# The opening loads, late values and second stacks of the projection reordered, and the last attention output finished in the next program

## The reference

```python
Q, K, V = split_heads(x @ Wq.T), split_heads(x @ Wk.T), split_heads(x @ Wv.T)
Q, K = rope(Q), rope(K)
probs = softmax(where(causal, Q @ K.T / sqrt(16), -inf))
x = layernorm(x + (probs @ V).merge_heads() @ Wo.T)

xf = layernorm(x) * ln_w + ln_b
expert = argmax(xf @ router_w); score = sigmoid(max(xf @ router_w))
xe = xf * score                                 # of the chosen expert only
routed = (silu(xe @ gate_w[e]) * (xe @ up_w[e])) @ down_w[e]
shared = (silu(xf @ sh_gate) * (xf @ sh_up)) @ sh_down
x = layernorm(x + (x + routed + shared))
```

## Time and profile before

| | us |
|---|---|
| median of 3 runs | 997.4 (996.0 to 997.84) |
| the profiled execution, its own time | 995.47 |
| its span from first to last instruction | 993.7 |
| busy PE, share of the span | 960.4, 97% |
| busy DVE | 738.8, 74% |
| busy ACT | 456.5, 46% |
| busy POOL | 364.4, 37% |

### The profile page before, as it was taken

How to read it: one execution, slowest core, us unless ns; L and a number is a source line. 1 busy time by engine, 2 the same in 40 slices (tenths; PEclk the granted TensorE clock), 3 DMA queues, 4 the chain that set the end, 5 groups by cost and what they waited for, 6 DMA issues and landing times. The chain is left out here.

```text
span 993.7 us, 19060 instructions
## 1 busy us (share of the span) xinstructions
PE 960.4 (97%) x6032; PEld 555.1 (56%) x6032; DVE 738.8 (74%) x1819; ACT 456.5 (46%) x639; POOL 364.4 (37%) x484
## 2 busy tenths in 40 slices
PE   7998899999999999999998799999999999999996
PEld 3556433343334333343333256666665899999996
DVE  4887899999999999999995556666666455655654
ACT  2453276667776676667766611222122233233231
POOL 7995232222222222222223124433334234433434
PEclk9999799999999999999999999999999999999999
DMA  8788434556665464755710187333334232222221
GB/s 295 179 234 197 75 55 61 60 76 84 95 93 75 61 102 61 103 75 73 156 18 8 17 258 244 87 81 81 80 115 167 70 93 79 74 80 78 77 72 44
DMA packets 176542, 100.17 MB, mean 101 GB/s; under 512 B 133856, under 2 KB 163168, under 8 KB 173120
## 3 DMA queue, kind: packets, MB, share of 16 engines
q1 hardware_dynamic: 162928, 72.66, 39.0%
q0 software_dynamic: 4944, 13.77, 3.9%
q10 hardware_dynamic: 8576, 12.58, 3.8%
HBM read 65.86 MB, written 32.70 MB: 99 GB/s over the span
## 5 line engine op out<-in xcount | busy, mean ns | idle before, releaser
L1037 ACT ACTIVATE probs<-scores_ps 128x1024 f32<-128x1024 f32 (+3 forms) x384 | 289.9, 807 | 118.4 <-PE scores_ps L978 115.7
L297 DVE TENSOR_REDUCE maxima<-max_ps 128x1 f32<-128x512 f32 (+2 forms) x352 | 228.2, 682 | 31.4 <-PE max_ps L255 20.8
L255 PE MATMUL max_ps<-k_stack,q_stack 96*128 96x512 bf16 (+3 forms) x768 | 224.1, 333 | 3.3 <-DVE maxima L292 0.5
L1140 POOL TENSOR_SCALAR_AFFINE_SELECT probs<-probs 128x512 f32<-128x512 f32 x128 | 81.3, 635 | 304.2 <-ACT probs L1037 303.4
L978 PE MATMUL scores_ps<-q_stack,k_stack 99*128 99x512 bf16 (+3 forms) x768 | 183.5, 328 | 3.5 <-PEq L355 1.7
L998 PE MATMUL out_ps<-probs,v_ones 128*32 128x512 f32 (+3 forms) x1536 | 163.6, 498 | 2.7 <-POOL probs L1140 2.2
L255 PEld LDWEIGHTS max_ps<-k_stack,q_stack 96*128 96x128 bf16 x768 | 74.5, 97 | 157.1 <-DVE maxima L297 58.7
L292 DVE CUSTOM_DVE_ANT_0 masked_out<-max_ps,mask_wide 128x384 bf16<-128x384 f32 (+1 forms) x256 | 149.2, 621 | 9.8 <-PE max_ps L255 6.1
L1425 ACT ACTIVATE silu<-gate_ps 128x512 f32<-128x512 f32 x71 | 42.4, 597 | 237.9 <-PE gate_ps L1344 140.6
L978 PEld LDWEIGHTS scores_ps<-q_stack,k_stack 99*128 99x128 bf16 x768 | 67.2, 98 | 66.2 <-ACT probs L1037 15.0
L1689 POOL DMA_INDIRECT out<-final,target_i x39 | 50.3, 1291 | 100.6 <-DVE final L1624 99.3
(11 more groups left out here) (163 smaller groups left out, 1211.9 us busy)
## 6 DMA issues: line engine op xcount, KB each, us to landing
k_stack<-k_parts SPq DMA_DIRECT2D x96, 128.0 KB, 4.3
q_stack<-q_parts SPq DMA_DIRECT2D x96, 128.0 KB, 7.4
q_parts<-parts SPq DMA_DIRECT2D x32, 192.0 KB, 3.2
k_parts<-parts SPq DMA_DIRECT2D x32, 192.0 KB, 3.2
sums_in<-expert_sums SPq DMA_DIRECT2D x39, 136.0 KB, 2.1
rows_in<-expert_rows SPq DMA_DIRECT2D x156, 32.0 KB
x_t<-in_x_cols SPq DMA_DIRECT2D x8, 512.0 KB, 11.2
heads_rows<-heads_out SPq DMA_DIRECT2D x128, 32.0 KB, 1.9
```

Source lines behind the costliest of these rows:

```text
L255: last = nc.tensor.matmul(part, self.q_stack[:ROWS, u.slot, h0 + k, t * P:(t + 1) * P], self.k_stack[:ROWS, u.slot, h0 + k, chunk * BLOCK: ...
L297: nc.vector.tensor_reduce(self.maxima[:, u.slot, chunk, h0:h0 + heads, t], self.bank("piece", u.i, n)[:, :heads * keys].rearrange("p (h k) ...
L1037: nc.scalar.activation(probs[:, s % RING, 2 * pair:2 * pair + 2, n0:], scores_ps[:, pair, :, n0:], ACT.Exp).then_inc(exp_done, 1)
L1140: nc.gpsimd.affine_select(out=tile, in_=tile, compare_op=ALU.is_ge, fill=0.0, base=0, pattern=[[0, GROUP], [1, P]], channel_multiplier=-1) ...
```

## The change

It touches the projection in five places, and the seam between `attend` and `feed`.

- First loads. x block 0 and Wq are loaded in halves by contraction chunk c, x and Wq in turn, each half with a semaphore of its own; then Wk, the half of the tables for Q, Wv, the half of the tables for K. `pair` runs its loops with c outside, and pair 0 waits for each half by itself. PE first does 8 matmuls of 128 columns on a zeroed tile `warm`, which DVE sets.
- ACT copies out values 7 and 8 before `mid(14)`, not between `high(15)` and `mid(15)`.
- The 12 stack loads of the second unit go out two at a time behind the stores of pairs 9 to 14, not behind all stores.
- DVE leaves the last 2 of the second unit's 13 early reductions to the start of `attend`.
- `send_neg` sends each of the three parts when it is made.
- `turn_out`, `normalise` and `store_heads` of the last output, and `make_tanh` and `make_score` of block 0, move to the start of `feed`. `final`, a tile of `feed`, now lies in `out_t`.

```diff
@@ send_neg
-        sp.wait_ge(self.neg_split, 4 * (u.i + 1))
-        for n in range(PARTS):
+        for n, steps in enumerate((1, 3, 4)):
+            sp.wait_ge(self.neg_split, 4 * u.i + steps)
@@ project
-    stacks_until = [min(max(0, 2 * (k - 2)), m.STACK_DMAS) if k > 2 else 0 for k in range(PAIRS)]
+    stacks_until = [min(max(0, 2 * (k - 2)), 2 * m.STACK_DMAS) for k in range(PAIRS)]
...
-            load_x(0)
-            sp.dma_start(w_qk[:, 0], io["Wq"].rearrange("(c p) o -> p c o", p=P)).then_inc(wq_in, 16)
-            sp.dma_start(tables[:, 0], io["tables"][:, 0]).then_inc(tables_in[0], 16)
+            for c in range(DC):
+                sp.dma_start(x_t[:, 0, c], x_cols[:, c, :BLOCK]).then_inc(x_half[c], 16)
+                sp.dma_start(w_qk[:, 0, c], io["Wq"][c * P:(c + 1) * P]).then_inc(wq_half[c], 16)
+            sp.dma_start(w_qk[:, 1], io["Wk"].rearrange("(c p) o -> p c o", p=P)).then_inc(wk_in, 16)
+            load_tables(0)
             sp.dma_start(w_v[:], io["Wv"].rearrange("(c p) o -> p c o", p=P)).then_inc(wv_in, 16)
-            sp.dma_start(w_qk[:, 1], io["Wk"].rearrange("(c p) o -> p c o", p=P)).then_inc(wk_in, 16)
+            load_tables(1)
...
-            m.load(sp, second, range(m.STACK_DMAS))
+            m.load(sp, second, range(stacks_until[-1] - m.STACK_DMAS, m.STACK_DMAS))
...
-                for e in range(2):
-                    for c in range(DC):
+                for c in range(DC):
+                    if k == 0:
+                        pe.wait_ge(x_half[c], 16)
+                        pe.wait_ge(wq_half[c], 16)
+                    for e in range(2):
...
+            pe.wait_ge(warm_made, 1)
+            for _ in range(8):
+                nc.tensor.matmul(v_ps[:, 0, 0, :P], warm[:], warm[:], start=True, stop=True)
...
-                late = k == PAIRS - 1
-                for n in values_after[k][:2] if late else values_after[k]:
+                for n in values_after[k] if k < PAIRS - 1 else ():
                     keep_v(n)
+                if k == PAIRS - 2:
+                    for n in values_after[PAIRS - 1][:2]:
+                        keep_v(n)
                 mid(k)
...
+            nc.vector.memset(warm[:], 0.0).then_inc(warm_made, 1)
...
-            m.reduce(dve, second, range(m.EARLY))
+            m.reduce(dve, second, range(m.EARLY - 2))
@@ attend
-            store_heads(Unit.number(UNITS - 1), 1)
...
-            f.make_tanh(act, 0, 0, 0)
...
+            m.reduce(dve, Unit.number(1), range(m.EARLY - 2, m.EARLY))
             each_unit(step)
             f.find_place(dve, 0, 0, 0)
-            turn_out(Unit.number(UNITS - 1), 1)
-            normalise(Unit.number(UNITS - 1), 1)
-            f.make_score(dve, 0, 0, 0)
@@ feed
-            for c in range(2):
-                sp.wait_ge(f.heads_stored[c], 16 * GROUP * UNITS)
+            sp.wait_ge(f.heads_stored[0], 16 * GROUP * (UNITS - 1))
+            sp.wait_ge(f.heads_stored[1], 16 * GROUP * (UNITS - 1))
...
                     f.load(sp, 2 * batch + 2, batch + 1, 0)
+                if isinstance(batch, int) and batch == 0:
+                    f.store_heads(sp, Unit.number(UNITS - 1), 1)
+                    sp.wait_ge(f.heads_stored[0], 16 * GROUP * UNITS)
+                    sp.wait_ge(f.heads_stored[1], 16 * GROUP * UNITS)
...
+            f.make_tanh(act, 0, 0, 0)
             f.scale_rows(act, 0, 0, 0)
...
             dve.wait_ge(total_zeroed, 1)
+            f.make_score(dve, 0, 0, 0)
             f.turn_heads(dve, 1, 0, 1)
+            f.turn_out(dve, Unit.number(UNITS - 1), 1)
+            f.normalise(dve, Unit.number(UNITS - 1), 1)
             by_batch(dve, step)
```

More of the change, by code:

```diff
@@ L367, in project @@
         v_ps = b.ps("v_ps", [P, 2, 2, D])
-        wq_in, wk_in, wv_in, wo_in = b.sem("wq_in"), b.sem("wk_in"), b.sem("wv_in"), b.sem("wo_in")
-        tables_in = [b.sem("tables_in0"), b.sem("tables_in1")]
+        warm = b.sb("warm", [P, P])
+        warm_made = b.sem("warm_made")
+        wk_in, wv_in, wo_in = b.sem("wk_in"), b.sem("wv_in"), b.sem("wo_in")
+        x_half = [b.sem(f"x_half{c}") for c in range(DC)]
+        wq_half = [b.sem(f"wq_half{c}") for c in range(DC)]
+        first_tables_in = [b.sem("q_tables_in"), b.sem("k_tables_in")]
+        tables_in = b.sem("tables_in")
         x_loaded = [b.sem(f"x_loaded{i}") for i in range(BLOCKS)]
@@ L411, in _ @@
                         sp.wait_ge(stored[r], 16 * GROUPS)
-                m.load(sp, first, stacks_after[k])
-            m.load(sp, second, range(m.STACK_DMAS))
+                for n in stacks_after[k]:
+                    m.load(sp, second if n >= m.STACK_DMAS else first, [n % m.STACK_DMAS])
+            m.load(sp, second, range(stacks_until[-1] - m.STACK_DMAS, m.STACK_DMAS))
             m.send_neg(sp, first)
@@ L519, in add @@
                                         ALU.add).then_inc(rot_ready, 1)
+            nc.vector.memset(warm[:], 0.0).then_inc(warm_made, 1)
             for k in range(PAIRS):
[L522 to L523 removed]
+                if k < 2:
+                    dve.wait_ge(first_tables_in[k], 16)
                 if k == 2:
[L525 removed]
+                    dve.wait_ge(tables_in, 16)
                 turn(k)
@@ L604, in __init__ @@
         self.heads_out = b.sb("heads_out", [P, 2, BLOCK // SQUARE, DK])
+        self.out_sb = b.sb("out_sb", [P, BLOCK])
+        self.out_t = b.sb("out_t", [P, BLOCK])
+        self.recip = b.sb("recip", [P, 2, BLOCK // SQUARE])
+        self.out_copied, self.out_turned, self.recip_done = b.sem("out_copied"), b.sem("out_turned"), b.sem("recip_done")
+        self.normed = keep["maxima"].normed
         self.heads_stored = [b.sem("heads_stored0"), b.sem("heads_stored1")]
@@ L656, in __init__, with turn_out, normalise, store_heads @@
         self.front_ps = self.route_ps = None
+    def turn_out(self, dve, u, c):
+        if u.i < 0:
+            return
+        k = 2 * u.i + c
+        dve.wait_ge(self.out_copied, k + 1)
+        wait(dve, self.normed, k)
+        self.nc.vector.transpose(self.out_t[:], self.out_sb[:]).then_inc(self.out_turned, 1)
+    def normalise(self, dve, u, c):
+        if u.i < 0:
+            return
+        nc = self.nc
+        k = 2 * u.i + c
+        dve.wait_ge(self.out_turned, k + 1)
+        wait(dve, self.heads_stored[c], 16 * GROUP * u.i)
+        rows = self.out_t[:].rearrange("p (b e) -> p b e", e=SQUARE)
+        nc.vector.reciprocal(self.recip[:, c], rows[:, :, DK]).then_inc(self.recip_done, 1)
+        dve.wait_ge(self.recip_done, k + 1)
+        nc.vector.tensor_tensor(self.heads_out[:, c], rows[:, :, :DK],
+                                self.recip[:, c].unsqueeze(2).to_broadcast([P, BLOCK // SQUARE, DK]),
+                                ALU.mult).then_inc(self.normed, 1)
+    def store_heads(self, sp, u, c):
+        if u.i < 0:
+            return
+        sp.wait_ge(self.normed, 2 * u.i + c + 1)
+        rows = self.scratch["heads"][u.i, c].rearrange("(b i) (h d) -> h i b d", i=SQUARE, h=GROUP)
+        for h in range(GROUP):
+            sp.dma_start(rows[h], self.heads_out[SQUARE * h:SQUARE * (h + 1), c]).then_inc(self.heads_stored[c], 16)
     def load(self, sp, i, batch, odd):
@@ L937, in load @@
                 m.load(sp, u, range(m.STACK_DMAS))
-            def store_heads(u, c):
-                if isinstance(u.i, int) and u.i < 0:
-                    return
-                sp.wait_ge(normed, 2 * u.i + c + 1)
-                rows = scratch["heads"][u.i, c].rearrange("(b i) (h d) -> h i b d", i=SQUARE, h=GROUP)
-                for h in range(GROUP):
-                    sp.dma_start(rows[h], heads_out[SQUARE * h:SQUARE * (h + 1), c]).then_inc(heads_stored[c], 16)
             def step(u):
@@ L959, in step @@
                     f.load(sp, odd, 0, odd)
-                store_heads(u.ahead(-1), 1)
-                store_heads(u, 0)
+                f.store_heads(sp, u.ahead(-1), 1)
+                f.store_heads(sp, u, 0)
                 m.send_neg(sp, u.ahead(1))
@@ L1044, in copy_out @@
                 wait(act, out_turned, 2 * u.i + c)
-                nc.scalar.copy(out_sb[:], out_ps[:]).then_inc(out_copied, 1)
+                nc.scalar.copy(f.out_sb[:], out_ps[:]).then_inc(out_copied, 1)
             def step(u):
@@ L1086, in step @@
                     if s == 2:
-                        turn_out(u.ahead(-1), 1)
+                        f.turn_out(dve, u.ahead(-1), 1)
                     if s == 4:
-                        normalise(u.ahead(-1), 1)
+                        f.normalise(dve, u.ahead(-1), 1)
                     if s == 6:
-                        turn_out(u, 0)
+                        f.turn_out(dve, u, 0)
                     if s == 7:
-                        normalise(u, 0)
+                        f.normalise(dve, u, 0)
                     if s == OWN_STEPS:
```

43 lines of the change are left out of this document (10 added, 33 removed).

## The result

| | before | after |
|---|---|---|
| median (4 runs each, side by side) | 997.28 us (996.0 to 997.84) | 981.61 us (980.75 to 983.3) |
| ratio | | 0.9847, 95% between 0.983 and 0.9864 |
| profiled execution, its own time | 995.47 | 980.75 |
| its span, mean granted clock of PE | 993.7, 0.988 | 979.0, 0.994 |

A forecast was written before the change was run, and what follows sets the result against it. PE, busy 97% of the span, was taken to bound the kernel; 2.8 + 3.7 + 1.1 + 3.5 + 2.0 = 13.1 us off the 997.4 median gave 984.3 us, own range 981 to 987, 8 in 10 within 980.5 to 989.5.

The forecast's parts named there:

- A: Opening of the projection: zero matmuls and halved loads start real work earlier and lose less to slow clock, gain 2.8 us.
- limit of 3.6 drawn from POOL: Opening: POOL's first split at 17.18 follows a memset ending at 13.58, so no more than 3.6 us can be gained.
- The second rival: Opening: halved loads land late, second halves at 6.4 or so; A gives 1.4, time 985.7 us, chance 0.05.
- B: Late values in the projection: earlier copies of values 7 and 8 remove PE's wait for ACT, gain 3.7 us.
- The third rival: Late values: the stall is replaced, value 9's copy comes 2 us later for PE; B gives 1.7, 986.3 us, chance 0.11.
- The second stacks: Second unit's stack loads in the projection: sent earlier by the reordering, they cost nothing and gain nothing of their own.
- the fifth rival: Pairs 9 to 14: the second stacks saturate the DMA engines and the kernel gets slower, say 1000 us, chance 0.03.
- C: Seam into `attend`: without the last two reductions the projection ends earlier, gain 1.1 us.
- D: Seam into `feed`: PE starts behind ACT's last copy, no longer behind SP's last store issue, gain 3.5 us.
- E: First gate and up groups of `feed`: the shorter pause may keep PE's faster clock, gain 2.0 us.
- the first rival: Opening and `feed` seam: the clock does not follow; A gives 1.5, E 0.5, time 987.1 us, chance 0.17.
- The fourth rival: `attend` takes up the first three gains; only D and E carry, giving 5.5 us, time 991.9 us, chance 0.04.

The follow-up runs named there:

- second set of runs: The changed kernel run again with no edit: median 982.94 us, ratio 0.9865 to the kernel before.

## Why the prediction was right, step by step

- **A, 2.8 forecast, 3.54 measured.** The mechanism holds, and both parts of the term were small by 0.3. Real work began at 4.70, not 5.0, because the zero matmuls took 3.78 us; the data could be used from 4.17 on. And the records lost 0.3 us, where the middle of the estimate had 0.6 and the far end 1.15. Over the ten traces with this opening A is 2.85 to 3.96, mean 3.4, and the records lose up to 1.0. The limit of 3.6 drawn from POOL was one of POOL alone: its first split comes 0.2 to 1.4 us behind its memset in these traces, since DVE waits for the tables' half. PE itself moves by more than 3.6 in three of them.
- **The second rival**, halves that land late, happened in part. In two of the ten traces PE waits for the second half of Wq (0.45 us until 6.69, and 0.36 until 7.12 in the one with the small matmuls at the seam), later than the 6.4 of the rival. The price was that wait, not the 1.4 us that the rival takes off A. By the prediction's own sign ("PE waits anywhere in 5 to 80") these traces would count against it, though they cost little. The whole loads were there at 5.42 and 5.48, so all of Wq came no sooner by halves. What was gained is the first half, there by 4.17. The Trainium skill ("DMA: Bandwidth & Descriptors", Bandwidth) advises DMAs of 1 MiB or more for bandwidth. For the bytes as a whole these two traces agree; for the part that PE waits for first, the smaller loads were the earlier ones.
- **B, 3.7 forecast, 3.71 measured.** The mechanism holds, and that the two numbers meet is partly luck. The wait for value 9's copy that was to take the place of the old one came, 1.0 us for 0.9. But DVE's banks were to hide half of it and hid none: DVE stood idle for 1.00 us too, and where that copy goes first, the 1.0 comes back whole. What made up for it are two short pauses of DVE behind the old stall, 0.65 and 0.19 us, that shrank to one of 0.26. In all DVE waited 5.1 us in this stage before and 1.5 now. `mid(15)` ends at 82.81, 2.9 us earlier than before, for 3.5 that PE had moved. The wait for value 9 follows this difference: it is 0.4 us in a trace where PE and POOL had both moved by 2.8, and 1.3 where PE had moved by 3.7 and POOL by 2.8. POOL moves less because DVE's first turn waits for the tables' half; whether an earlier load of it would take the 1.0 away is not tested. The third rival, 2 us of stall, is out. The run with the old order of copies gives the price of the step back.
- **The second stacks, cost 0.** Right. The last two are issued at 86.28 and nobody waits for one. The DMA engines are full there (a share of 1.01 and 0.94 in 80 to 88), yet neither ACT nor POOL waits for a store in the projection, so the fifth rival never began. The cover was worth 2.4 us.
- **C, 1.1 forecast, 1.12 measured**, and 1.11 by the run that undoes it. From DVE's last reduction in the projection to the scores is 0.7 us.
- **D, 3.5 forecast, 3.64 measured.** From ACT's copy to the gate group it is 0.51 us, where 0.67 was taken over from SP's case. The last to come is ACT's copy, as foretold, and the work that moved is paid by nobody: DVE turns the output at 558.87, behind the turn of block 1's heads, long before PE's product is ready for it.
- **E, 2.0 forecast, 2.27 measured.** The level was kept across the pause of 1.16 us in the profiled execution. But in two of the eleven traces with the same pause, the ones without zero matmuls and with whole loads, the gate group took 3.4 us, and from it to the next it was 8.66 us: 0.57 less than before the change, near the 0.8 and 0.5 that the forecast had for this case. So this part of the first rival, at 0.17, is not refuted: it happens in some executions. The forecast weighed the two outcomes and put 2.0 between them, which is the mean of these eleven traces too; that the kept value came out in this one is luck.
- **What the sum left out.** 0.73 us in `attend` goes with the slow stretch behind 104, 6.8 us long in one trace of the changed kernel and 10.2 in the other. The 13.1 of the forecast against the 14.7 of the traces is 0.7 in A, 0.3 in E, 0.1 in D, and 0.7 here, less 0.3 given back in the rest of `feed`, whose cause is open.
- **The range.** The lower bounds of the five terms add up to a gain of 7.5, not 7.3; it changes the far end by 0.2 us and nothing else.
- **The median.** The forecast took the profiled execution of before to lie 1.9 us under the median, which held (995.47 against 997.28), and put the same distance on the result, where it was 0.9. By the second set of runs the median is 982.9, 2.2 above that execution. What the sum can't know is the state of the clock; the two traces of the changed kernel differ by 2.4 us by it.
- **Only the last seam carries.** The fourth rival falls by the positions: what A, B and C had gained at the first scores, 8.37 us, is still there at ACT's last copy (9.10) and at the end (14.7 with D and E). The runs without B and without the second stacks' reordering lose by the ratios too; for A and C the medians alone could not tell.

## What to carry to other kernels

Read a seam by who comes last, take that away, and then step through to who comes last next; that gave four terms out of five within 0.3 us here, one of them with two errors that cancel. A pause of the bounding engine costs its own length and often the slower clock behind it, so it can pay to fill one that can't be removed with matmuls that nobody reads (about 1.2 us in the opening, 2.2 at the last seam), if they fit into it at the slower level too. When an early part is made faster, list what was covered by its slowness (here the second unit's stacks, 2.4 us) and move it in the same change.

## What was not expected of the hardware

- A short pause is followed by the slower level in some executions and not in others. Behind 1.16 us the gate group took 3.4 us in two traces and 1.95 or 1.96 in nine; in the two, the column of the granted clock falls 0.3 and 0.4 us after the group has begun. Behind 4.80 us it took 3.75 both times. In the opening, where the zero matmuls still ran at the slower level, the records behind a pause of 0.57 us took 9.01 us for the 7.19 to 8.03 without one (one trace).
- A stage in which PE has gaps of 0.2 to 0.6 us, since DVE bounds it, ran 6.8 to 10.2 us at the slower level in every trace without added matmuls. With zero matmuls in the gaps it was none in one trace and 3.4 us in the other. In front of the first scores this costs nothing while DVE binds (7.08 and 7.10 us from the combine to the scores with 3.3 and 4.6 us of it); inside `attend` the slow time, with another 3.4 us between 522 and 529 in three traces, goes with up to 3 us.
- The runs of one kernel lie up to 5.8 us apart at a mean granted clock of 0.990 to 0.994 (whole loads, 981.06 to 986.88), and within 1.6 at 0.996 to 0.999. The clock is not all of it: other kernels had runs within 0.7 and 1.4 us at 0.990 to 0.994.
